# Routing: ScalarE scales x to unit length, and the normalised mu carries the router's scalar

## The chip, the cores and the metric

The kernel runs on one core of one Trainium2 chip. The metric is the device time of one execution in microseconds (us), the median over the runs. A core has five engines that work independently and wait for each other on semaphores: TensorE (PE in the profile, its weight loads PEld), VectorE (DVE), ScalarE (ACT), GpSimd (POOL) and SyncE (SP), which issues DMAs.

## The reference

Sixteen sequences of 256 tokens with 256 features pass through attention, a feed-forward block, a second attention, and a soft mixture of 16 experts with 16 slots each. Only the routing of the last block is touched by the change:

```python
xn = _layernorm(x, ln_gamma, ln_beta)
x_unit = _l2norm(xn, axis=-1)          # x / max(|x|, 1e-12)
mu_unit = _l2norm(mu, axis=0)
logits = jnp.einsum('bnd,des->bnes', x_unit * scale, mu_unit)
dispatch = jax.nn.softmax(logits, axis=1)
combine = jax.nn.softmax(logits.reshape(B, N, E * S), axis=-1).reshape(B, N, E, S)
slot_in = jnp.einsum('bnd,bnes->besd', xn, dispatch)
```

`scale` is one scalar. Here B = 16, N = 256, D = 256, E * S = 256.

## The kernel before, in words

The kernel is a row of stages: prologue, attention, feed-forward, attention, then `route`, `experts` and `combine`. All engines meet at a barrier between stages. `route` goes through the 16 sequences ("batches") one after another; the order of the work on each engine is written out by hand, and semaphores tie the engines together. A batch has its 256 tokens in two halves (q = 0, 1) of 128 partitions x 256 features.

For one batch the work goes through these tiles:

- VectorE: `ln.statistics` (route_stats, route_mean_var); GpSimd: `ln.inverse_deviation` (route_var_eps, route_rstd); VectorE: `ln.normalise` (route_xn, L351, two operations from SBUF to SBUF).
- GpSimd: `affine` (route_xg = xn * gamma, route_xa = xg + beta); ScalarE: `square` (route_sq with its sum); GpSimd: `lengths` (route_length, then route_length_min, L1744).
- VectorE: `unit`: route_inv_length, the reciprocal (L1641), then route_xu = xa * inv_length * scale (L1645, two operations from SBUF to SBUF).
- TensorE transposes xu (L1513). ScalarE rounds it to route_xT_hi (L1589), VectorE takes the rest, route_xT_lo (L1651). Every product on TensorE is made in three passes of such high and low parts.
- TensorE: `logits` for k = 0 (dispatch) and k = 1 (combine). VectorE: `maxima` (route_top, L1656); ScalarE: `exponentials` (route_ex, L1595); VectorE: `invert` (route_rinv) and `weigh` (route_weight, L1667).
- TensorE transposes the weights. ScalarE copies them: route_disp_hi (L1609) and moe_comb (L1614). VectorE: route_disp_lo (L1680). ScalarE and GpSimd split xa: `round_x` (route_xaS_hi) and `split_x` (route_xaS_lo, L1748). TensorE: `slot_inputs` (L1544). ScalarE: moe_slots (L1624).

The stages of this chain overlap over several batches. In one pass of a body, batch f is in front (logits and softmax), batch f - 1 at the back (dispatch and slots), batch f + 1 gets xu and xT, batch f + 2 gets xn, xa and its length, batch f + 3 its statistics. The bodies of f = 0 to 2 and of 13 to 16 stand outside the hardware loop, which runs two of them at a time for f = 3 to 12. The last bodies leave out the parts for batches that don't exist. Each engine's order in a body:

- VectorE: normalise (f + 2), maxima (f, 0), unit (f + 1), disp_lo (f - 1), statistics (f + 3), invert (f, 0), maxima (f, 1), xT_lo (f + 1), weigh (f, 0), invert (f, 1), weigh (f, 1).
- ScalarE: disp_hi (f - 1), exponentials (f, 0), comb (f - 1), xT_hi (f + 1), exponentials (f, 1), square (f + 2), slots (f - 1), round_x (f + 1).
- GpSimd: split_x (f), affine (f + 2), inverse_deviation (f + 3), lengths (f + 2).
- TensorE: logits (f, 0), transposed weights (f - 1), logits (f, 1), transposed x (f + 1), slot_inputs (f - 1).

Ahead of the bodies, mu is normalised once: VectorE builds the diagonal matrix route_mu_diag (L1707, two operations) from the identity and 1/|mu|, TensorE multiplies it with ones, so that every partition has the whole row of 1/|mu|, and VectorE multiplies mu with that row.

Of the kernel before, what the change touches and what calls it, by code (L numbers as in the profile page):

```python
# [49 lines left out]
def at_least(eng, sem, value):  # L50

    if not isinstance(value, int) or value > 0:
        eng.wait_ge(sem, value)
# [1386 lines left out]
def route(nc, d, st):  # L1440
# [7 lines left out]
    with ExitStack() as stack:  # L1448
# [126 lines left out]
        @block.scalar  # L1575
        def _(act):
            def square(f, i):

                act.wait_ge(xa_ready, f + 1)
                for q in range(NC):  # L1580
                    at_least(act, sumsq_ready, NC * f + q)
                    at_least(act, len_ready, f)
                    nc.scalar.activation(sq[:, :], xa[i][:, q, :], ACT.Square, accum_out=sumsq[:, q:q + 1]).then_inc(sumsq_ready, 1)

            def transposed_x(f, i):
                for c in range(DC):
                    act.wait_ge(xt_psum, DC * f + c + 1)
                    at_least(act, l_psum, 2 * (f - 1))
                    nc.scalar.copy(xT[i][0][:, c, :], x_bank[c][:, 0:N]).then_inc(xt_hi, 1)  # L1589

            def exponentials(f, k):
                act.wait_ge(top_ready, 2 * f + k + 1)
                at_least(act, weight_ready, 4 * (f - 1) + 2 * k + 2)
                for r in range(2):
                    nc.scalar.activation(ex[k][:, r, :], l_bank[k][:, r * ES:(r + 1) * ES], ACT.Exp,  # L1595
                                         bias=top[k][:, r:r + 1], accum_out=rsum[k][:, r:r + 1]).then_inc(ex_ready, 1)

            def round_x(f, i):

                at_least(act, i_psum, f - 1)  # L1600
                act.wait_ge(xa_ready, f + 1)
                nc.scalar.copy(xaS[i][0][:, :, :], xa[i][:, :, :]).then_inc(xas_hi, 1)

            def batch(f, i, front, back, following, later, latest):
                g = f - 1
                if back:
                    act.wait_ge(t_psum, 2 * g + 1)
                    at_least(act, i_psum, g)
                    nc.scalar.copy(disp[0][:, :, :], t_bank[0][:, :].rearrange("p (q n) -> p q n", q=NC)).then_inc(disp_hi, 1)  # L1609
                if front:  # L1610
                    exponentials(f, 0)
                if back:
                    act.wait_ge(t_psum, 2 * g + 2)
                    nc.scalar.copy(st.comb[:, :, bass.ds(g, 1), :].rearrange("p j b n -> p (j b) n"),  # L1614
                                   t_bank[1][:, :].rearrange("p (j n) -> p j n", j=EC)).then_inc(comb_stored, 1)
                if following:
                    transposed_x(f + 1, 1 - i)
                if front:
                    exponentials(f, 1)
                if later:  # L1620
                    square(f + 2, i)
                if back:
                    act.wait_ge(i_psum, g + 1)
                    nc.scalar.copy(st.slots[:, :, bass.ds(g, 1), :].rearrange("p c b n -> p (c b) n"),  # L1624
                                   i_bank[:, :].rearrange("p (c n) -> p c n", c=DC)).then_inc(slots_stored, 1)
                if following:
                    round_x(f + 1, 1 - i)

            square(0, 0)
            transposed_x(0, 0)  # L1630
            square(1, 1)
            round_x(0, 0)
            batch_pairs_ahead(act, batch)

        @block.vector
        def _(dve):
            def unit(f, i):

                dve.wait_ge(lmin_ready, f + 1)
                at_least(dve, xu_ready, NC * f)  # L1640
                nc.vector.reciprocal(inv_length[:, :], length_min[:, :]).then_inc(inv_ready, 1)  # L1641
                dve.wait_ge(inv_ready, f + 1)
                at_least(dve, xt_psum, DC * f)
                for q in range(NC):
                    nc.vector.tensor_scalar(xu[:, q, :], xa[i][:, q, :], inv_length[:, q:q + 1], scale[:, 0:1],  # L1645
                                            ALU.mult, ALU.mult).then_inc(xu_ready, 1)

            def transposed_x(f, i):
                for c in range(DC):
                    dve.wait_ge(xt_hi, DC * f + c + 1)  # L1650
                    nc.vector.tensor_tensor(xT[i][1][:, c, :], x_bank[c][:, 0:N], fp32_of(xT[i][0][:, c, :]),  # L1651
                                            ALU.subtract).then_inc(xt_lo, 1)

            def maxima(f, k):
                dve.wait_ge(l_psum, 2 * f + k + 1)
                nc.vector.tensor_reduce(top[k][:, :], l_bank[k][:, :].rearrange("p (r n) -> p r n", r=2), AX,  # L1656
                                        ALU.max, negate=True).then_inc(top_ready, 1)

            def invert(f, k):
                dve.wait_ge(ex_ready, 4 * f + 2 * k + 2)  # L1660
                nc.vector.reciprocal(rinv[k][:, :], rsum[k][:, :]).then_inc(rinv_ready, 1)

            def weigh(f, k):
                dve.wait_ge(rinv_ready, 2 * f + k + 1)
                at_least(dve, t_psum, 2 * (f - 1) + k + 1)
                for r in range(2):
                    nc.vector.tensor_scalar(weight[k][:, r, :], ex[k][:, r, :], rinv[k][:, r:r + 1], None,  # L1667
                                            ALU.mult).then_inc(weight_ready, 1)

            def batch(f, i, front, back, following, later, latest):  # L1670
                g = f - 1
                if later:
                    ln.normalise(dve, f + 2, xg_ready, 1)
                if front:
                    maxima(f, 0)
                if following:
                    unit(f + 1, 1 - i)
                if back:
                    dve.wait_ge(disp_hi, g + 1)
                    nc.vector.tensor_tensor(disp[1][:, :, :], t_bank[0][:, :].rearrange("p (q n) -> p q n", q=NC),  # L1680
                                            fp32_of(disp[0][:, :, :]), ALU.subtract).then_inc(disp_lo, 1)
                if latest:
                    ln.statistics(dve, f + 3)
                if front:
                    invert(f, 0)
                if front:
                    maxima(f, 1)
                if following:
                    transposed_x(f + 1, 1 - i)
                if front:  # L1690
                    weigh(f, 0)
                if front:
                    invert(f, 1)
                    weigh(f, 1)

            nc.vector.tensor_tensor(mu_sq[:, :, :], mu_raw[:, :, :], mu_raw[:, :, :], ALU.mult).then_inc(mu_step, 1)
            ln.statistics(dve, 0)
            dve.wait_ge(mu_psum, 1)
            nc.vector.tensor_copy(mu_sum[:, :], i_bank[:, 0:EC]).then_inc(mu_step, 1)
            ln.normalise(dve, 0, xg_ready, 1)  # L1700
            ln.statistics(dve, 1)

            dve.wait_ge(mu_pow, 2)
            nc.vector.reciprocal(mu_inv[:, :], mu_max[:, :]).then_inc(mu_step, 1)
            dve.wait_ge(mu_step, 3)
            for j in range(EC):
                last = nc.vector.tensor_scalar(mu_diag[:, j, :], st.ident[:, :], mu_inv[:, j:j + 1], None, ALU.mult)  # L1707
            last.then_inc(mu_step, 1)
            ln.normalise(dve, 1, xg_ready, 1)
            dve.wait_ge(mu_psum, 2)  # L1710
            nc.vector.tensor_tensor(mu_unit[:, :, :], mu_raw[:, :, :], l_bank[0][:, 0:ES].unsqueeze(1).to_broadcast([P, DC, ES]),
                                    ALU.mult).then_inc(mu_step, 1)
            dve.wait_ge(mu_step, 5)
            nc.vector.tensor_copy(mu[0][:, :, :], mu_unit[:, :, :]).then_inc(mu_step, 1)
            dve.wait_ge(mu_step, 6)
            nc.vector.tensor_tensor(mu[1][:, :, :], mu_unit[:, :, :], fp32_of(mu[0][:, :, :]), ALU.subtract).then_inc(mu_ready, 1)
            dve.wait_ge(in_, 48)
            ln.statistics(dve, 2)
            unit(0, 0)
            transposed_x(0, 0)  # L1720
            batch_pairs_ahead(dve, batch)

# [378 lines left out]
```

## Time and profile before

| | |
|---|---|
| median of 3 runs | 1213.59 us (1213.54, 1213.59, 1218.73) |
| profiled execution, its own time | 1216.6 us |
| its span | 1214.8 us |
| TensorE busy | 1047.5 us, 86% |
| VectorE busy | 894.0 us, 74% |
| ScalarE busy | 734.7 us, 60% |
| GpSimd busy | 439.4 us, 36% |
| granted TensorE clock, mean | 0.925 |
| routing stage | about 964 to 1119 us of the span |

The busy shares are means over all stages. A group of instructions is one line of the kernel with its output and inputs; its busy time is the sum of its instructions' durations. An instruction's duration contains the time for which it stands in the engine, whatever holds it there. Rows of one tile that follow each other directly are merged: "2.34 DVE ... x2" are two instructions that together take 2.34 us from the start of the first to the end of the second. In brackets stands how long the engine was idle before, and what released it.

### The profile page before, as it was taken

Reading aid. Unit: us, or ns where it says so; the run is one execution under the profiler, and the core shown is the slowest. Engines: PE = TensorE matmul, PEld = TensorE weight load, DVE = VectorE, ACT = ScalarE, POOL = GpSimd, SP = SyncE. Lnnn points to the kernel's source line nnn. Section 1 sums busy time; section 2 is a strip of 40 time slices with the busy share of each in tenths; the row PEclk is TensorE's granted clock in tenths of the full one; section 3 lists DMA queues with packets and bytes.
Section 4 is the critical chain, followed back from the end, with each engine's and each line's share of the span. In section 5 each row is a group of like instructions: output and inputs, shape, how many; then the busy total and the mean of one; then the engine's idle time right before and its main releaser. Section 6 shows DMA issues by size and latency. Waiting matters only on the chain. (4 is left out here: it accounts for less than half of the span.)

```text
span 1214.8 us, 28495 instructions
## 1 busy us (share of the span) xinstructions
PE 1047.5 (86%) x8053; PEld 998.5 (82%) x8053; DVE 894.0 (74%) x2324; ACT 734.7 (60%) x2481; POOL 439.4 (36%) x753
## 2 busy tenths in 40 slices
PE   6779999999999998799999917888888657777998
PEld 6679999999999998799999916888778646777777
DVE  3567667777767775677777647899998579996656
ACT  3466666676666665433333318899999346666754
POOL 0222323222232321121212126667776457663015
PEclk9889999999999999899999967899999769989559
DMA  7678970000000000000000045555664100000113
GB/s 223 144 134 227 130 117 0 0 0 0 0 0 0 0 1 1 31 1 0 0 0 0 0 108 150 150 159 161 175 172 128 19 1 1 0 0 2 42 35 121
DMA packets 71574, 73.90 MB, mean 61 GB/s; under 512 B 23024, under 2 KB 63828, under 8 KB 71380
## 3 DMA queue, kind: packets, MB, share of 16 engines
q1 hardware_dynamic: 70692, 72.47, 24.3%
q10 hardware_dynamic: 816, 0.66, 0.2%
q8 instruction: 28, 0.46, 0.2%
q14 instruction: 38, 0.31, 0.1%
HBM read 41.52 MB, written 31.54 MB: 60 GB/s over the span
## 5 line engine op out<-in xcount | busy, mean ns | idle before, releaser
L776 POOL TENSOR_TENSOR att_prob<-att_ex,att_rinv 128x308 f32<-128x308 f32 x128 | 90.0, 703 | 215.8 <-DVE att_rinv L679 202.5
L1056 ACT ACTIVATE att_ex<-att_s_bank,att_mx 128x77 f32<-128x77 f32 x512 | 144.3, 347 | 14.2 <-DVE att_mx L1122 12.7
L1338 ACT ACTIVATE ffn_hid<-ffn_h_bank,ffn_b 128x256 f32<-128x256 f32 x128 | 60.8, 476 | 125.5 <-DVE ffn_hT_lo L1369 64.8
L638 ACT ACTIVATE att_ex<-att_s_bank,att_mx 128x77 f32<-128x77 f32 x512 | 125.1, 333 | 11.5 <-DVE att_mx L669 11.4
L702 DVE TENSOR_TENSOR att_pT_lo<-att_t_bank,att_pT_hi 128x512 fp32r<-128x512 f32 x128 | 88.3, 690 | 33.2 <-ACT att_pT_hi L616 32.9
L646 ACT ACTIVATE att_qT<-att_q_bank 128x256 f32<-128x256 f32 x128 | 49.2, 385 | 100.3 <-PE att_q_bank L496 99.1
L1196 POOL TENSOR_TENSOR att_prob<-att_ex,att_rinv 128x256 f32<-128x256 f32 x128 | 80.3, 628 | 72.1 <-DVE att_rinv L1137 72.0
L516 PE MATMUL att_s_bank<-att_keys,att_qT 128*128 128x154 f32 x512 | 95.1, 309 | 0.0
L616 ACT CAST att_pT_hi<-att_t_bank 128x512 fp32r<-128x512 f32 x128 | 75.0, 587 | 24.6 <-PE att_t_bank L526 19.8
L540 PE MATMUL att_o_bank<-att_pT_hi,att_vals_hi 128*128 128x256 f32 x256 | 83.0, 324 | 3.0 <-DVE att_oT_lo L683 2.0
L1309 PE MATMUL ffn_o_bank<-ffn_w_hi,ffn_hT_hi 128*128 128x256 f32 x256 | 74.4, 291 | 7.6 <-DVE ffn_hT_lo L1369 7.6
L967 PE MATMUL att_s_bank<-att_ks,att_qs 100*128 100x154 f32 x256 | 52.6, 290 | 31.6 <-ACT att_ex L1056 20.9
L683 DVE TENSOR_TENSOR att_oT_lo<-att_o_bank,att_oT_hi 128x256 fp32r<-128x256 f32 x128 | 54.3, 424 | 33.3 <-ACT att_oT_hi L651 29.6
L496 PE MATMUL att_q_bank<-att_xT_hi,att_wq_hi 128*128 128x256 f32 x256 | 75.3, 294 | 2.9 <-DVE att_xT_lo L662 2.9
L526 PE MATMUL att_t_bank<-all_ident,att_prob 128*128 128x128 f32 x512 | 76.9, 273 | 0.0
L1296 PE MATMUL ffn_h_bank<-ffn_xT_hi,ffn_w_hi 128*128 128x256 f32 x256 | 72.8, 284 | 3.5 <-DVE ffn_xT_lo L1356 3.5
L1122 DVE TENSOR_REDUCE att_mx<-att_s_bank 128x4 f32<-128x308 f32 x128 | 59.7, 467 | 20.6 <-PE att_s_bank L967 20.2
L516 PEld LDWEIGHTS att_s_bank<-att_keys,att_qT 128*128 128x128 f32 x512 | 73.4, 193 | 1.1
L496 PE MATMUL att_q_bank<-att_xT_hi,att_wq_lo 128*128 128x256 f32 x256 | 73.1, 286 | 0.0
L496 PE MATMUL att_q_bank<-att_xT_lo,att_wq_hi 128*128 128x256 f32 x256 | 72.8, 284 | 0.0
L967 PEld LDWEIGHTS att_s_bank<-att_ks,att_qs 100*128 100x128 f32 x256 | 41.9, 204 | 37.4 <-DMA att_qs<-q_dram 29.1
L1296 PE MATMUL ffn_h_bank<-ffn_xT_lo,ffn_w_hi 128*128 128x256 f32 x256 | 72.5, 283 | 0.0
(275 smaller groups left out, 4162.6 us busy)
## 6 DMA issues: line engine op xcount, KB each, us to landing
att_qs<-q_dram SPq DMA_DIRECT2D x96, 128.0 KB, 2.8
ks_dram<-att_zeros SPq DMA_DIRECT2D x16, 462.0 KB, 5.7
att_ks<-ks_dram SPq DMA_DIRECT2D x16, 462.0 KB, 5.0
all_x<-in_x SPq DMA_DIRECT2D x4, 1024.0 KB, 7.1
att_vd<-vd_dram SPq DMA_DIRECT2D x16, 256.0 KB
q_dram<-att_qT_hi SPq DMA_DIRECT2D x16, 256.0 KB, 2.1
q_dram<-att_qT_lo SPq DMA_DIRECT2D x16, 256.0 KB, 2.1
out<-comb_y SPq DMA_DIRECT2D x16, 256.0 KB, 2.1
```

The lines of the kernel that those rows point to most:

```text
L496: last = nc.tensor.matmul(q_bank[c % 2][:, 0:N], wq[a][:, k, c * P:(c + 1) * P], xT[b][:, k, :], start=n == 0, stop=n == 5)
L516: last = nc.tensor.matmul(out, qT[c % 2][:, q * P:(q + 1) * P], keys[:, kc, h0:h0 + 2, :], start=first, stop=True)
L526: last = nc.tensor.transpose(t_bank[t % 2][:, h * N + q * P:h * N + (q + 1) * P], prob[:, q, (2 * t + h) * SK:(2 * t + h) * SK + P], st.id ...
L540: last = nc.tensor.matmul(o_bank[j % 2][:, 0:N], vals[a][:, v * P:(v + 1) * P], pT[t % 2][b][:, h * N:(h + 1) * N], start=t % PC == 0 and ...
L616: nc.scalar.copy(pT[t % 2][0][:, :], t_bank[t % 2][:, :]).then_inc(pt_hi, 1)
L638: last = nc.scalar.activation(ex[t % RING][:, r, :], s_bank[t % 2][:, r * SK:(r + 1) * SK], ACT.Exp, bias=mx[t % 2][:, r:r + 1])
L702: nc.vector.tensor_tensor(pT[t % 2][1][:, :], t_bank[t % 2][:, :], fp32_of(pT[t % 2][0][:, :]), ALU.subtract).then_inc(pt_lo, 1)
L776: nc.gpsimd.tensor_tensor(out, e, w, ALU.mult).then_inc(p_ready, 1)
L967: last = nc.tensor.matmul(s_bank[t % 2][:, q * PAIR:(q + 1) * PAIR], qs[i][0:ROWS, t, q * P:(q + 1) * P], ks[i][0:ROWS, t // 4, t % 4, :, ...
L1056: last = nc.scalar.activation(ex[t % RING][:, r, :], s_bank[t % 2][:, r * SK:(r + 1) * SK], ACT.Exp, bias=mx[t % 2][:, r:r + 1], **total)
L1196: nc.gpsimd.tensor_tensor(main, e[:, :, :, 0:MAIN], w.to_broadcast([P, NC, 2, MAIN]), ALU.mult).then_inc(p_ready, 1)
L1296: last = nc.tensor.matmul(h_bank[t % 4][:, 0:N], w1[a][:, k, t, :], xT[b][:, k, :], start=n == 0, stop=n == 5)
```

## The change

Three things change in `route`. The reciprocal stays on VectorE as `invert_length` and moves from behind the first maxima to the head of VectorE's body, ahead of normalise. The product with it goes to ScalarE as `unit`, two operations at the head of ScalarE's body, ahead of disp_hi. The router's scalar leaves this product: mu_diag is multiplied by it once, so VectorE waits for the small inputs' DMA ahead of mu_diag instead of ahead of the statistics of batch 2.

```diff
@@ ScalarE
+            def unit(f, i):
+                act.wait_ge(inv_ready, f + 1)
+                at_least(act, xt_psum, DC * f)
+                for q in range(NC):
+                    nc.scalar.mul(xu[:, q, :], xa[i][:, q, :], inv_length[:, q:q + 1]).then_inc(xu_ready, 1)
...
             def batch(f, i, front, back, following, later, latest):
                 g = f - 1
+                if following:
+                    unit(f + 1, 1 - i)
                 if back:
                     act.wait_ge(t_psum, 2 * g + 1)
...
             square(0, 0)
+            unit(0, 0)
             transposed_x(0, 0)
@@ VectorE
-            def unit(f, i):
+            def invert_length(f):
 
                 dve.wait_ge(lmin_ready, f + 1)
                 at_least(dve, xu_ready, NC * f)
                 nc.vector.reciprocal(inv_length[:, :], length_min[:, :]).then_inc(inv_ready, 1)
-                dve.wait_ge(inv_ready, f + 1)
-                at_least(dve, xt_psum, DC * f)
-                for q in range(NC):
-                    nc.vector.tensor_scalar(xu[:, q, :], xa[i][:, q, :], inv_length[:, q:q + 1], scale[:, 0:1],
-                                            ALU.mult, ALU.mult).then_inc(xu_ready, 1)
...
             def batch(f, i, front, back, following, later, latest):
                 g = f - 1
+                if following:
+                    invert_length(f + 1)
                 if later:
                     ln.normalise(dve, f + 2, xg_ready, 1)
                 if front:
                     maxima(f, 0)
-                if following:
-                    unit(f + 1, 1 - i)
...
             dve.wait_ge(mu_step, 3)
+            dve.wait_ge(in_, 48)
             for j in range(EC):
-                last = nc.vector.tensor_scalar(mu_diag[:, j, :], st.ident[:, :], mu_inv[:, j:j + 1], None, ALU.mult)
+                last = nc.vector.tensor_scalar(mu_diag[:, j, :], st.ident[:, :], mu_inv[:, j:j + 1], scale[:, 0:1],
+                                               ALU.mult, ALU.mult)
...
-            dve.wait_ge(in_, 48)
             ln.statistics(dve, 2)
-            unit(0, 0)
+            invert_length(0)
             transposed_x(0, 0)
```

## Rows read from the trace of the kernel before

**Rows 1.** Busy us by stretch: PE, PEld, DVE, ACT, POOL, granted clock, DMA share, GB/s

```profile
984.00:1110.00 126.00, 96.46 (x696) 89.44 (x696) 115.90 (x288) 79.74 (x262) 80.17 (x98) 0.92 0.00 1
```

**Rows 2.** Groups by form, 975 to 1120: busy us, mean ns, idle before

```profile
L1645 DVE TENSOR_SCALAR route_xu<-route_xa,route_inv_length,route_scale 128x256 f32<-128x256 f32 x32 | 35.7, 1154 | 0.6
...
L1583 ACT ACTIVATE route_sq<-route_xa 128x256 f32<-128x256 f32 x30 | 12.5, 416 | 0.5
...
L1589 ACT CAST route_xT_hi<-route_x_bank 128x256 fp32r<-128x256 f32 x32 | 10.6, 375 | 31.0 <-PE route_x_bank L1513 30.8
```

**Rows 3.** Waits from 984 to 1110: us in total, times, longest

```profile
DVE route_inv_length L1641 <- POOL route_length_min L1744: 2.4, 7, 0.5
```

**Rows 4.** Timeline of VectorE, 1034 to 1062: start, duration in us

```profile
1036.90 0.17 DVE L1641 RECIPROCAL route_inv_length<-route_length_min 128x2 f32<-128x2 f32 x1 [0.36 <-POOL route_length_min L1744]
1037.10 2.34 DVE L1645 TENSOR_SCALAR route_xu<-route_xa,route_inv_length,route_scale 128x256 f32<-128x256 f32 x2
1039.36 0.68 DVE L1680 TENSOR_TENSOR route_disp_lo<-route_t_bank,route_disp_hi 128x512 fp32r<-128x512 f32 x1
...
1041.64 0.74 DVE L1651 TENSOR_TENSOR route_xT_lo<-route_x_bank,route_xT_hi 128x256 fp32r<-128x256 f32 x2
...
1045.62 2.68 DVE L1645 TENSOR_SCALAR route_xu<-route_xa,route_inv_length,route_scale 128x256 f32<-128x256 f32 x2
1048.22 0.68 DVE L1680 TENSOR_TENSOR route_disp_lo<-route_t_bank,route_disp_hi 128x512 fp32r<-128x512 f32 x1
```

**Rows 5.** Timeline of GpSimd, batches 0 and 1, and three in the loop

```profile
984.41 1.28 POOL L1748 TENSOR_TENSOR route_xaS_lo<-route_xa,route_xaS_hi 128x512 fp32r<-128x512 f32 x1
...
993.39 0.22 POOL L1744 TENSOR_SCALAR route_length_min<-route_length 128x2 f32<-128x2 f32 x1
...
1036.56 0.22 POOL L1744 TENSOR_SCALAR route_length_min<-route_length 128x2 f32<-128x2 f32 x1 [0.29 <-ACT route_xaS_hi L1602]
1036.73 1.29 POOL L1748 TENSOR_TENSOR route_xaS_lo<-route_xa,route_xaS_hi 128x512 fp32r<-128x512 f32 x1
1037.98 1.31 POOL L1729 TENSOR_TENSOR route_xg<-route_xn,route_gamma 128x512 f32<-128x512 f32 x1
...
1045.06 0.22 POOL L1744 TENSOR_SCALAR route_length_min<-route_length 128x2 f32<-128x2 f32 x1 [0.29 <-POOL route_length L1741]
1045.60 1.28 POOL L1748 TENSOR_TENSOR route_xaS_lo<-route_xa,route_xaS_hi 128x512 fp32r<-128x512 f32 x1 [0.32 <-issue]
...
1053.95 0.22 POOL L1744 TENSOR_SCALAR route_length_min<-route_length 128x2 f32<-128x2 f32 x1 [0.29 <-ACT route_xaS_hi L1602]
```

**Rows 6.** Timeline of ScalarE: second exponentials of a batch, and disp_hi

```profile
1041.84 0.47 ACT L1595 ACTIVATE route_ex<-route_l_bank,route_top 128x256 f32<-128x256 f32 x1 [1.15 <-DVE route_top L1656]
...
1044.69 0.59 ACT L1609 CAST route_disp_hi<-route_t_bank 128x512 fp32r<-128x512 f32 x1
```

**Rows 7.** Timeline of VectorE, start of the stage and batches 0 and 1

```profile
969.25 0.48 DVE L1707 TENSOR_SCALAR route_mu_diag<-all_ident,route_mu_inv 128x128 f32<-128x128 f32 x2
973.79 0.73 DVE L351 TENSOR_SCALAR route_xn<-all_x,route_mean_var,route_rstd 128x256 f32<-128x256 f32 x2 [4.06 <-POOL route_rstd L343]
...
984.48 1.68 DVE L351 TENSOR_SCALAR route_xn<-all_x,route_mean_var,route_rstd 128x256 f32<-128x256 f32 x2 [2.71 <-POOL route_rstd L343]
986.09 0.68 DVE L1656 TENSOR_REDUCE route_top<-route_l_bank 128x2 f32<-128x512 f32 x1
...
986.87 2.13 DVE L1645 TENSOR_SCALAR route_xu<-route_xa,route_inv_length,route_scale 128x256 f32<-128x256 f32 x2
...
989.84 0.67 DVE L1656 TENSOR_REDUCE route_top<-route_l_bank 128x2 f32<-128x512 f32 x1
...
994.20 0.69 DVE L1656 TENSOR_REDUCE route_top<-route_l_bank 128x2 f32<-128x512 f32 x1 [1.13 <-PE route_l_bank L1523]
...
997.50 0.68 DVE L1680 TENSOR_TENSOR route_disp_lo<-route_t_bank,route_disp_hi 128x512 fp32r<-128x512 f32 x1
```

**Rows 8.** Timeline of VectorE, body 14, near the stage's end

```profile
1105.62 0.69 DVE L1656 TENSOR_REDUCE route_top<-route_l_bank 128x2 f32<-128x512 f32 x1 [2.16 <-PE route_l_bank L1523]
```

## The prediction

> **What bounds the kernel now.** I read the page first, then the busy time by stretch, then the groups and waits of the routing stage, and last its timeline engine by engine. The page's busy shares are a mean over stages with different limits, and its chain that ended last lies wholly in the combine stage at the end, so neither says anything about routing. The stretch from 984 to 1110 us does: VectorE is busy 115.9 of 126 us, TensorE 96.5, GpSimd 80.2, ScalarE 79.7 [rows 1]. VectorE is the full engine there, and its largest group in the stage is the very product that is to leave it: 32 operations, 35.7 us, 1154 ns each in the mean [rows 2]. A ScalarE operation on a tile of the same 128x256 takes 375 to 416 ns [rows 2].
>
> Why 1154 ns? The timeline tells. At 1037.10 two such products start; they end at 1039.44, 2.34 us for the pair [rows 4], while GpSimd runs route_xaS_lo from 1036.73 to 1038.02 and then route_xg to 1039.29 [rows 5]. The pair ends 0.15 us after GpSimd's second operation. The next batch repeats it: start 1045.62 against GpSimd's 1045.60, 2.68 us [rows 4, 5]. The pair at 986.87, with less cover from GpSimd, takes 2.13 us [rows 7]. So the product stands behind GpSimd: each of its two operations lasts until one of GpSimd's 1.3 us operations is over. The same befalls route_xn, another VectorE product from SBUF to SBUF: beside the route_xaS_lo of 984.41 to 985.69 its pair takes 1.68 us and ends 0.47 us after it [rows 7].
>
> The Trainium skill ("SBUF — State Buffer", Who interferes with whom) says that VectorE's two-port operations and GpSimd's take one shared pair of ports as an exclusive lock, and that issue order decides who blocks. The overlaps just read agree with it.
>
> **The loop that repeats.** route_disp_lo starts at 1039.36; the second maximum and xT_lo follow; ScalarE's second exponentials start at 1041.84 [rows 4, 6]; then ScalarE's squares, GpSimd's length, and its minimum route_length_min at 1045.06, route_xaS_lo at 1045.60, and the next disp_lo at 1048.22 [rows 4, 5]. Minimum to minimum is 8.50 us, then 8.89 [rows 5], 8.70 in the mean. disp_lo starts 1.34 us after route_xaS_lo ends in both (1038.02 to 1039.36, 1046.88 to 1048.22), because the product's pair ends 0.15 us after route_xg. The reciprocal route_inv_length already waits for that minimum in 7 batches, though two other VectorE operations, xn and the first maximum, stand ahead of it [rows 3].
>
> **Part 1, the product leaves VectorE.** Two operations a batch, 35.7 us in all. What that is worth is not 35.7 us but what the loop gives back, below.
>
> **Part 2, the reciprocal goes to the head of VectorE's batch.** Behind it wait xn, the first maximum, disp_lo and statistics, and everything after them. The minimum comes when it came before, since ScalarE's squares and GpSimd's order ahead of it are untouched. In the loop the reciprocal starts 0.34 us after the minimum's start (1036.56 to 1036.90) [rows 4, 5], so xn starts at about +0.5 (all such times count from the start of route_length_min), and GpSimd's route_xaS_lo starts at +0.17 (1036.73) or +0.54 (1045.60) [rows 5]. xn now lies where the product lay, and is held by the same operation. It is held once only: route_xg reads xn and can't start before it. From the row at 984.48, the pair ends 0.47 us after route_xaS_lo; the maximum starts 0.07 before that end (986.09), lasts 0.68, and the operation behind it can start 0.08 before it ends [rows 7]. disp_lo therefore starts 0.47 - 0.07 + 0.68 - 0.08 = 1.00 us after route_xaS_lo instead of 1.34: **0.34 us a batch**. VectorE will stand idle for some 1.6 us at the head of each batch: the 0.3 us by which it waits now [rows 3], and the 1.3 us that xn and the maximum, about 0.65 each to the next operation, now fill.
>
> **Part 3, ScalarE gets the product.** The trace has no ScalarE product with a scale per partition from SBUF. Bounds: route_xT_hi at 375 ns below, route_ex, which has a bias per partition, at 470 above [rows 2, 6]; I take 0.45, 0.9 us for the pair (the value between them that is nearer to the one with an operand per partition). It starts when the reciprocal is over, at +0.6, so ends at +1.5. disp_hi, now behind it, takes 0.59 [rows 6], to +2.1. disp_lo needs it at +0.17 + 1.29 + 1.00 = +2.46: hidden, with 0.35 us to spare. The exponentials then wait for the first maximum, which ends at +2.5. They (0.95), the copy of the combine weights (0.6) and the first half of xT_hi (0.35) end at about +4.4; xT_lo wants that half at 2.46 + 2.28 = +4.74 [rows 4], and the second exponentials want ScalarE at 2.46 + 2.48 = +4.94 [rows 4, 6]: hidden, 0.3 us to spare. TensorE's transposes get xu two us earlier, which gains nothing, as the slot products behind them wait for disp_lo. If the cover were gone the pair would cost its 0.9 us a batch.
>
> The Trainium skill ("ScalarE: Activation LUTs", What ACT_TABLE_LOAD costs) gives an operation with one pointer operand about 280 ns + 0.833 ns an element. An estimate from it is 0.49 us, 0.08 more for the pair than by the rows, and still covered.
>
> **Part 4, the scalar on mu.** Two operations on route_mu_diag get a second scalar; 0.48 us for both as now. They start at 969.25 and also wait for a DMA that is now waited for later. VectorE's next operation waits for GpSimd 4.06 us until 973.79 [rows 7]; so even if the DMA lands 4 us later than the two operations now start, that wait covers it. I take 0.
>
> **Start and end of the stage.** Batch 0: the product (986.87, 2.13 us) falls away between the maximum (ends 986.77) and the statistics; the second maximum, at 989.84, then has only to wait for the first exponentials, which follow the first maximum at 986.8 and take 0.95. It starts at about 987.95: 1.9 us [rows 7]. Batch 1: the minimum of 993.39 [rows 5], 1.9 us earlier, is at about 991.5, its route_xaS_lo ends 0.17 + 1.28 later at 992.95, disp_lo can start at 993.95 instead of 997.50 [rows 7]. TensorE's first logits, for which the maximum of 994.20 waited [rows 7], are done 1.9 us earlier too, by 992.3, and don't hold it. That is 3.5 us in all after batch 1, and that wait of 1.13 us is the larger part of the second step. Batches 2 to 13: 12 x 0.34 = 4.1. In batches 14 to 16 there is no xn and TensorE is the bound: the maximum at 1105.62 waited 2.16 us for it [rows 8], so nothing more comes.
>
> **Sum.** 3.5 + 4.1 = 7.6 us. The profiled execution took 1216.6 (span 1214.8, 1.8 around it) and would take 1209.0; it lies 3.0 over the median of the runs, 1213.59, from which I get **1206.0**. It is -0.63%; a measurement of this kernel can tell about 0.5% (6.1 us) from no change.
>
> **Rivals.** *A, 0.60: the forecast above*, with its own range of 1203 to 1209 (0.2 to 0.45 a batch, 2.5 to 4.5 at the start).
> *B, 0.17: the gain of the steady batches is eaten* and only the start remains, 1210, no change. ScalarE's chain through the first exponentials to xT_hi has 0.3 us of slack in my sum. If ScalarE or TensorE (whose transposes feed xT_hi, and which has spells at the low clock) is later by 0.3 + 0.34 us than I count, xT_lo moves past where it is now and the 12 x 0.34 are gone. For it: in the stage TensorE is granted 0.92 of its clock, not all of it [rows 1]. Against it: ScalarE's operations follow each other without gaps when their inputs are there.
> *C, 0.15: more gain, 1201.5.* In every second batch xn (+0.5) and route_xaS_lo (+0.54) are a tie [rows 5]; in it the product at 1045.62 lost. If xn starts first and is then not held, its pair takes some 0.74 us, disp_lo waits only for disp_hi at +2.1 instead of +2.82, and 6 batches gain 0.7 more: 4.3 us. Against it: in the tie at 1045.60 GpSimd's operation kept its 1.28 us and VectorE's waited, and route_xaS_lo can still slip in between the two operations of xn and hold the second one. (The Trainium skill, the same section as above: whoever issues first holds the pair for its whole instruction.)
> *D, 0.08: slower, 1223.* ScalarE's product is itself held by GpSimd as VectorE's was. With the 2.68 us of the longest pair [rows 4] xu ends at 0.6 + 2.68 = +3.3 and disp_hi at +3.9, so disp_lo starts at +3.9 where it now starts at +2.80; 12 batches lose 1.1 us each, the start gives 3.5, 1213.6 + 13.2 - 3.5 = 1223. It decides where the pair takes 2.4 us, 1.2 an operation: disp_lo at +3.6, 9.6 - 3.5 = 6.1 us lost. Against it: ScalarE's square of the same tile has a mean of 416 ns over 30 [rows 2].
>
> Faster by over 0.5%: four fifths of A and all of C, 0.62. Within: the rest of A, B, 0.30. Slower: 0.08. The range 1200 to 1212 takes in A, B and most of C, and leaves out D.
>
> **What would show it.** xu on ScalarE at 0.40 to 0.50 us, gapless pair. On VectorE: the reciprocal waits for the minimum in nearly every batch, about 1.5 us; xn's pair takes 1.5 to 1.7 us wherever it overlaps route_xaS_lo, and disp_lo starts 1.0 us after that ends. Minimum to minimum 8.35 us in the mean. The second maximum of batch 0 at 988. The prediction is wrong if xn isn't held (C), if xT_lo waits for xT_hi (B), or if the product on ScalarE lasts over 1 us (D).

## The result, and the profile after

The changed kernel is faster by 0.6%: ratio to before 0.9939, 95% interval 0.9925 to 0.9953, with medians of 1210.27 us against 1217.36 us over 20 runs each. (Two of the three runs of before that the prediction had, and so their median, lay at the lower end of those 20.) The forecast was 0.63% and 1206.0 us. On a second chip the ratio was 0.9912 (0.9894 to 0.9931); the two intervals just overlap.

The profiled execution has a span of 1206.2 us (before 1214.8) and took 1208.0. To see what the routing stage itself does, I take its length as the time from GpSimd's first operation in it (route_ones) to TensorE's first in the experts' stage (exp_b_bank): 1111.48 - 964.01 = 147.5 us after, 1120.15 - 964.60 = 155.6 us before. The stage is 8.1 us shorter and accounts for all of the gain but 0.6 us, which lies ahead of it. This length is a finer measure than the whole time. In the 13 profiles of this study the stage begins anywhere from 958.8 to 967.4 us, although nothing ahead of it was changed.

Busy time in the stretch that answers to [rows 1] (PE, PEld, DVE, ACT, POOL, granted clock, DMA share, GB/s):

```profile
984.00:1102.00 118.00, 90.84 (x699) 82.61 (x699) 92.46 (x258) 91.64 (x291) 79.49 (x97) 0.99 0.00 1
```

No engine is full any more. VectorE fell from 92% to 78%, ScalarE rose from 63% to 78%. The granted clock of TensorE rose too, from 0.92 to 0.99, and could be thought to be what gains. It doesn't set the loop: in the kernel before, two batches take 17.42 us at a granted clock of 1.00 (the minima of 1019.14 and 1036.56) and 17.40 at 0.90 (1045.06 and 1062.46). It does touch the last bodies: in that profile the granted clock is 0.50 from 1102 to 1104 us, the lower of its two levels, after TensorE had been busy for only 0.5 of the 2 us from 1098, and VectorE then waits 2.16 us for TensorE's logits [rows 8]. Experiment 1 has the same loop, a granted clock of 1.00 there and a wait of 0.52 us, and from the last minimum to the stage's end it takes 14.7 us in place of 15.7. About 1 us of the 8.1 may thus be that spell and not the change. The groups of the stage (busy us, mean ns of one, idle before), first xn's of the kernel before, then three of after:

```profile
L351 DVE TENSOR_SCALAR route_xn<-all_x,route_mean_var,route_rstd 128x256 f32 x20 | 7.3, 409 | 0.3
...
L351 DVE TENSOR_SCALAR route_xn<-all_x,route_mean_var,route_rstd 128x256 f32 x20 | 15.0, 790 | 0.8
L1589 ACT ACTIVATE route_xu<-route_xa,route_inv_length 128x256 f32<-128x256 f32 x32 | 14.6, 502 | 16.4 <-DVE route_inv_length L1650 16.4
...
L1650 DVE RECIPROCAL route_inv_length<-route_length_min 128x2 f32<-128x2 f32 x16 | 2.6, 164 | 22.9 <-POOL route_length_min L1749 22.9
```

The product that lasted 1154 ns on VectorE [rows 2] lasts 502 on ScalarE. But xn, which in the loop lasted 409 ns, now lasts 790, and VectorE stands idle for 22.9 us ahead of the reciprocal, where it waited 2.4 us before [rows 3]. VectorE's timeline shows where both come from:

```profile
1031.21 0.17 DVE L1650 RECIPROCAL route_inv_length<-route_length_min 128x2 f32<-128x2 f32 x1 [1.60 <-POOL route_length_min L1749]
1031.40 1.41 DVE L351 TENSOR_SCALAR route_xn<-all_x,route_mean_var,route_rstd 128x256 f32 x2
1032.73 0.68 DVE L1660 TENSOR_REDUCE route_top<-route_l_bank 128x2 f32<-128x512 f32 x1
1033.33 0.68 DVE L1684 TENSOR_TENSOR route_disp_lo<-route_t_bank,route_disp_hi 128x512 fp32r<-128x512 f32 x1
...
1039.38 0.17 DVE L1650 RECIPROCAL route_inv_length<-route_length_min 128x2 f32<-128x2 f32 x1 [1.70 <-POOL route_length_min L1749]
1039.67 1.63 DVE L351 TENSOR_SCALAR route_xn<-all_x,route_mean_var,route_rstd 128x256 f32 x2
1041.23 0.68 DVE L1660 TENSOR_REDUCE route_top<-route_l_bank 128x2 f32<-128x512 f32 x1
1041.83 0.67 DVE L1684 TENSOR_TENSOR route_disp_lo<-route_t_bank,route_disp_hi 128x512 fp32r<-128x512 f32 x1
```

And GpSimd's, with which it is to be read:

```profile
1030.87 0.22 POOL L1749 TENSOR_SCALAR route_length_min<-route_length 128x2 f32<-128x2 f32 x1 [0.29 <-ACT route_xaS_hi L1608]
1031.05 1.28 POOL L1753 TENSOR_TENSOR route_xaS_lo<-route_xa,route_xaS_hi 128x512 fp32r<-128x512 f32 x1
1033.08 1.27 POOL L1734 TENSOR_TENSOR route_xg<-route_xn,route_gamma 128x512 f32<-128x512 f32 x1 [0.75 <-DVE route_xn L351]
...
1039.03 0.22 POOL L1749 TENSOR_SCALAR route_length_min<-route_length 128x2 f32<-128x2 f32 x1 [0.29 <-POOL route_length L1746]
1039.56 1.28 POOL L1753 TENSOR_TENSOR route_xaS_lo<-route_xa,route_xaS_hi 128x512 fp32r<-128x512 f32 x1 [0.31 <-issue]
1041.58 1.26 POOL L1734 TENSOR_TENSOR route_xg<-route_xn,route_gamma 128x512 f32<-128x512 f32 x1 [0.75 <-DVE route_xn L351]
...
1047.57 0.22 POOL L1749 TENSOR_SCALAR route_length_min<-route_length 128x2 f32<-128x2 f32 x1 [0.29 <-ACT route_xaS_hi L1608]
```

route_xaS_lo ends at 1032.33 and at 1040.84. xn's pair ends 0.48 and 0.46 us later, disp_lo starts 1.00 and 0.99 us later, in place of 1.34 before [rows 4, 5]. From minimum to minimum it is 8.16 and 8.54 us, 8.35 in the mean, in place of 8.70.

### The profile page after: what moved, and what is told of

Its sections match the earlier page's. It is cut to its first block and busy times, and to the rows that moved or that the text cites. A ratio compares the mean times of both kernels' runs of the same rounds, so it can differ in the third digit from the quotient of the medians.

```text
span 1206.2 us, 28505 instructions
## 1 busy us (share of the span) xinstructions
PE 1040.5 (86%) x8053; PEld 988.6 (82%) x8053; DVE 874.2 (72%) x2292; ACT 748.9 (62%) x2513; POOL 437.8 (36%) x753
```

## The experiments

The theory under test, below the **loop theory**: a batch lasts as long as the loop that runs from route_length_min over whatever VectorE has beside GpSimd's 1.3 us operations, then disp_lo, the second maxima, ScalarE's exponentials and squares, back to the next minimum; a tensor_scalar of VectorE from SBUF to SBUF (the products, xn, the weights) that meets one of them is held until that is over. The rivals are that the time follows the engines' load (work taken off the full engine is what gains, wherever it stands), that ScalarE is the new bound, and that the early reciprocal is what gains. The kernels of a group shared a chip and its runs of before: changed again, 1, 2 and 3; then 4 to 7; then 9, 7 again and 8. "Stage" is the length defined above, "two batches" the time between every second route_length_min in the loop (before 17.39 us); for 8, 9 and the second run of 7 it is taken from one route_length to the second after it, which has the same period.

| kernel | ratio to before, 95% | stage us | two batches us |
|---|---|---|---|
| before | 1 | 155.6 | 17.39 |
| changed, again | 0.9912 (0.9894 to 0.9931) | 147.5 | 16.70 |
| 1 only the scalar moves | 0.9988 (0.9969 to 1.0007) | 154.0 | 17.39 |
| 2 reciprocal back behind the maxima | 0.9880 (0.9862 to 0.9899) | 140.1 | 15.45 |
| 3 route_xaS_lo behind route_xg | 0.9878 (0.9858 to 0.9898) | 143.2 | 16.13 |
| 4 ScalarE's product behind the exponentials | 1.0046 (1.0027 to 1.0065) | 161.9 | 18.40 |
| 5 ScalarE's product made twice | 0.9952 (0.9934 to 0.9970) | 150.7 | 17.06 |
| 6 as 2, product behind the exponentials | 0.9814 (0.9793 to 0.9836) | 134.2 | 14.24 |
| 7 as 2, product behind disp_hi | 0.9818 (0.9794 to 0.9841) | 131.7 | 14.24 |
| 7 again | 0.9806 (0.9781 to 0.9831) | 132.5 | 14.23 |
| 8 as 7, minimum on VectorE | 0.9821 (0.9802 to 0.9839) | 135.7 | 14.28 |
| 9 before, both at the head of VectorE | 1.0011 (0.9993 to 1.0029) | 156.8 | 17.98 |

### The changed kernel again

> The changed kernel itself, to have it on the same chip as the next three. 0.61% faster than before, about 7.5 us, under every theory; it is the mark for the others.

The stage is 147.5 us long, as in the first profile; the ratio is 0.3% lower than there. So 8 of the about 10.7 us (0.9912 of 1215.5) are the stage's; the other 2.7 lie in stages that both kernels have alike, and I don't claim them for the change.

### Experiment 1: the scalar alone

```diff
-nc.vector.tensor_scalar(xu[:, q, :], xa[i][:, q, :], inv_length[:, q:q + 1], scale[:, 0:1],
-                        ALU.mult, ALU.mult).then_inc(xu_ready, 1)
+nc.vector.tensor_scalar(xu[:, q, :], xa[i][:, q, :], inv_length[:, q:q + 1], None,
+                        ALU.mult).then_inc(xu_ready, 1)
```

(and the changed kernel's lines for mu_diag)

> Kernel before, in which only the scalar has moved into mu_diag; VectorE keeps the product, with one scalar operand instead of two. Loop theory (a batch lasts from one route_length_min over route_xaS_lo, the held product, disp_lo and the second maxima to the next): no change, within 0.2% of before, since the product's pair ends with GpSimd's route_xg and not by its own work; the pair stays at 2.1 to 2.7 us in the loop. Rival, that the second scalar operand makes the product slow: the pair falls towards 0.74 us and the kernel gains as much as the whole change or more.

No change: 0.9988, the interval holds 1. Two batches take 17.39 us as before; the stage is 1.6 us shorter, 1.0 of it behind the last minimum, where the kernel before had its spell at the low clock, and 0.3 ahead of the first. The product with one scalar lasts as long as with two:

```profile
L1645 DVE TENSOR_SCALAR route_xu<-route_xa,route_inv_length 128x256 f32<-128x256 f32 x32 | 36.5, 1181 | 0.6
```

The second operand is not what makes it slow, and this part of the change gives nothing in the loop and nothing that the whole time can show.

### Experiment 9: the place alone

```diff
 def batch(f, i, front, back, following, later, latest):      # VectorE, before
     g = f - 1
+    if following:
+        unit(f + 1, 1 - i)
     if later:
         ln.normalise(dve, f + 2, xg_ready, 1)
     if front:
         maxima(f, 0)
-    if following:
-        unit(f + 1, 1 - i)
```

> Kernel before, in which only the place has changed: reciprocal and product, both still on VectorE, stand at the head of its body, ahead of xn and the first maximum. Loop theory: the product's first operation is held by route_xaS_lo, its second is free, because route_xg now waits for the xn behind it; the pair falls to about 1.6 us, ends 0.47 us after route_xaS_lo, then xn (0.65) and the maximum (0.60) come into the loop: disp_lo starts 1.7 us after route_xaS_lo ends instead of 1.34. 0.3 us a batch lost, 12 batches 4 us, less what the start gives or takes: 0.1 to 0.5% slower than before. So the early place alone costs, and the gain of the change is that of ScalarE's taking the product. Rival, that starting the reciprocal early is what gains: 0.3 to 0.6% faster than before.

The ratio, 1.0011, can't be told from 1; the loop can. Two batches take 17.98 us (from 1040.93 to 1058.91; before 17.39), so 0.3 us a batch are lost, as expected. The product's pair is here beside route_xaS_lo alone and is held once; xn behind it has no GpSimd operation beside it and takes its own 0.72 us:

```profile
1041.28 0.17 DVE L1641 RECIPROCAL route_inv_length<-route_length_min 128x2 f32<-128x2 f32 x1 [1.70 <-POOL route_length_min L1744]
1041.48 1.72 DVE L1645 TENSOR_SCALAR route_xu<-route_xa,route_inv_length,route_scale 128x256 f32<-128x256 f32 x2
1043.13 0.72 DVE L351 TENSOR_SCALAR route_xn<-all_x,route_mean_var,route_rstd 128x256 f32 x2
```

route_xaS_lo ran from 1041.46 to 1042.73 there, the pair ended 0.47 us later; its mean over the stage is 755 ns in place of 1154. 0.3 us a batch, lost twelve times, is 3.6 us; the stage is only 1.2 us longer, as the start gains 2.9 (in the bodies of f = 0 and 1 the minima come 8.4 and 8.1 us apart in place of 10.3 and 9.2). The early reciprocal by itself doesn't gain in the loop: that rival is out.

### Experiment 2: the reciprocal back behind the maxima

```diff
 def batch(f, i, front, back, following, later, latest):      # VectorE, changed
     g = f - 1
-    if following:
-        invert_length(f + 1)
     if later:
         ln.normalise(dve, f + 2, xg_ready, 1)
     if front:
         maxima(f, 0)
+    if following:
+        invert_length(f + 1)
```

> Changed kernel, with the reciprocal put back behind the first maxima (the product stays on ScalarE). Loop theory: xn and the first maximum again fill the wait for route_length_min and no longer overlap route_xaS_lo, so xn's pair falls to 0.74 us; disp_lo then waits only for disp_hi, at +2.1 after the minimum's start instead of +2.46 and +2.80. 0.5 us a batch, 6 us, so 1.1% faster than before and minimum to minimum about 7.85 us. Rival, that the whole gain is the work taken off VectorE wherever the reciprocal stands, or that ScalarE is what bounds the changed kernel: the same time as the changed kernel, 0.6% faster than before.

1.2% faster than before, 0.3% more than the changed kernel on the same chip, and the stage 7.4 us shorter than the changed kernel's; two batches take 15.45 us, 7.73 for one where 7.85 were expected. VectorE's timeline of one batch:

```profile
1050.97 0.73 DVE L351 TENSOR_SCALAR route_xn<-all_x,route_mean_var,route_rstd 128x256 f32 x2
1051.62 0.68 DVE L1660 TENSOR_REDUCE route_top<-route_l_bank 128x2 f32<-128x512 f32 x1
1052.59 0.17 DVE L1650 RECIPROCAL route_inv_length<-route_length_min 128x2 f32<-128x2 f32 x1 [0.29 <-POOL route_length_min L1749]
1054.29 0.69 DVE L1684 TENSOR_TENSOR route_disp_lo<-route_t_bank,route_disp_hi 128x512 fp32r<-128x512 f32 x1 [1.53 <-ACT route_disp_hi L1617]
```

ScalarE's timeline of the same batch:

```profile
1052.88 0.91 ACT L1589 ACTIVATE route_xu<-route_xa,route_inv_length 128x256 f32<-128x256 f32 x2 [0.90 <-DVE route_inv_length L1650]
1053.69 0.56 ACT L1617 CAST route_disp_hi<-route_t_bank 128x512 fp32r<-128x512 f32 x1
```

xn and the maximum are done before the minimum, xn at its own 0.73 us. Now disp_lo waits 1.53 us for disp_hi, which stands behind ScalarE's product: the next wait in the row, at +2.05 after the minimum of 1052.24. The instructions of every engine are those of the changed kernel, so the theory that load alone counts is out.

### Experiment 3: route_xaS_lo behind route_xg

```diff
 def batch(f, i, front, back, following, later, latest):      # GpSimd, changed; affine in two
+    if later:
+        scaled(f + 2)        # route_xg
     if front:
         split_x(f, i)        # route_xaS_lo
     if later:
-        affine(f + 2, i)
+        shifted(f + 2, i)    # route_xa
```

> Changed kernel, with GpSimd's route_xaS_lo moved from ahead of route_xg to between route_xg and route_xa. route_xg needs xn, so GpSimd runs nothing large beside xn. If xn is held by GpSimd's operation, its pair falls from 1.4 to 1.7 us to 0.74 us, and disp_lo waits only for disp_hi at +2.1: 0.3 to 0.5 us a batch, 4 to 6 us, 0.9 to 1.1% faster than before; part may be lost again as route_xa ends later, which ScalarE's squares read. If xn is slow for itself (two scalar operands, its place), the pair stays at 1.4 us or more and the time at that of the changed kernel or slower.

1.2% faster than before, the stage 4.3 us shorter than the changed kernel's. The loop gains 0.28 us a batch on the changed kernel's, a little less than the 0.3 to 0.5 expected; the ratio is over the expected one because the changed kernel's is on this chip as well. VectorE's order is untouched, and xn's pair is free at once; the weights are held in its place:

```profile
1048.17 1.03 DVE L1671 TENSOR_SCALAR route_weight<-route_ex,route_rinv 128x256 f32<-128x256 f32 x2
...
1051.62 0.17 DVE L1650 RECIPROCAL route_inv_length<-route_length_min 128x2 f32<-128x2 f32 x1 [1.69 <-POOL route_length_min L1755]
1051.92 0.74 DVE L351 TENSOR_SCALAR route_xn<-all_x,route_mean_var,route_rstd 128x256 f32 x2
```

This is the cleanest test of the hold: the same instruction in the same place of VectorE's row, 0.74 us without GpSimd beside it and 1.41 to 1.63 with. The weights' pair went from 0.61 to 1.03 us, since GpSimd's route_xa (1047.52 to 1048.79) now ran beside it. The Trainium skill ("SBUF — State Buffer", Who interferes with whom) names tensor_scalar among the VectorE operations whose two-port modes can take the pair of ports shared with GpSimd. This trace agrees for the two tensor_scalars here, xn and the weights.

### Experiment 4: ScalarE's product behind the exponentials

```diff
 def batch(f, i, front, back, following, later, latest):      # ScalarE, changed
-    if following:
-        unit(f + 1, 1 - i)
...
     if front:
         exponentials(f, 0)
+    if following:
+        unit(f + 1, 1 - i)
```

> Changed kernel, with ScalarE's product moved from the head of its body to behind the first exponentials; the reciprocal stays at VectorE's head. Loop theory: the exponentials still wait for the held xn and the maximum (until +2.5), xu ends at +4.3, TensorE's transposes at +5.0, xT_hi's first half at +5.4 where xT_lo wants it at +4.74; a batch lasts 0.6 to 0.8 us longer, 8 to 10 us, so the gain is gone: between 0.2% slower and 0.1% faster than before. Rival, that only the load of the engines counts: the same time as the changed kernel.

Slower than before, 1.0046 (1.0027 to 1.0065): more than expected. Two batches take 18.40 us in the mean, 0.85 us a batch over the changed kernel where 0.6 to 0.8 were forecast. The place of the wait is the expected one:

```profile
1055.57 0.85 DVE L1655 TENSOR_TENSOR route_xT_lo<-route_x_bank,route_xT_hi 128x256 fp32r<-128x256 f32 x2 [0.90 <-ACT route_xT_hi L1595]
```

So ScalarE's product is hidden in the changed kernel by its place, not by ScalarE's having room.

### Experiment 5: ScalarE's product made twice

```diff
     for q in range(NC):
         nc.scalar.mul(xu[:, q, :], xa[i][:, q, :], inv_length[:, q:q + 1]).then_inc(xu_ready, 1)
+    for q in range(NC):
+        nc.scalar.mul(spare[:, q, :], xa[i][:, q, :], inv_length[:, q:q + 1])
```

> Changed kernel, with ScalarE's two products made once more into a spare tile, right behind the first two and ahead of disp_hi (nobody reads them). It measures the cover over ScalarE's product. Loop theory: 0.85 us more ahead of disp_hi, which ends at +2.9 instead of +2.05, so disp_lo at +2.95 instead of +2.46 and +2.80: 0.15 to 0.5 us a batch, 4 us, 0.3% slower than the changed kernel; half of the added work is covered. If ScalarE is the bound: all 16 x 0.85 = 13 us come on top, 0.5% slower than before. If ScalarE has room: no change against the changed kernel.

The stage is 3.2 us longer than the changed kernel's, two batches 17.06 in place of 16.70 us, 0.18 a batch. (The changed kernel wasn't run on this chip, so the stages are compared and not the ratios.) 16 x 0.8 = 13 us were added to ScalarE, and three quarters of it cost nothing. ScalarE doesn't bound the changed kernel, but the cover over disp_hi is thin: in the changed kernel disp_hi ends at 1032.80 and disp_lo starts at 1033.33, 0.5 us to spare where 0.35 were summed. With 0.8 us more, disp_lo waits for disp_hi in one of two batches:

```profile
1048.87 0.69 DVE L1687 TENSOR_TENSOR route_disp_lo<-route_t_bank,route_disp_hi 128x512 fp32r<-128x512 f32 x1 [0.21 <-ACT route_disp_hi L1620]
```

The minimum there is at 1046.11, so disp_lo starts at +2.76 in place of +2.46; in the other batch it is +2.85 in place of +2.80.

### Experiments 6 and 7: both moves together

Experiment 2's VectorE, with ScalarE's product behind the first exponentials (6) or right behind disp_hi (7).

```diff
 def batch(f, i, front, back, following, later, latest):      # ScalarE, experiment 7
-    if following:
-        unit(f + 1, 1 - i)
...
+    if following:
+        unit(f + 1, 1 - i)
     if front:
         exponentials(f, 0)
```

> The last two together: reciprocal behind the first maxima, ScalarE's product behind the first exponentials. Loop theory: the first maximum is done before the minimum, disp_hi at -0.3, disp_lo at +0.55 instead of +2.46 and +2.80, exponentials +0.2 to +1.15, xu to +2.0, xT_hi to +3.5, second exponentials at +3.5 instead of about +5.1. The chain alone gives 6.7 us from minimum to minimum; GpSimd's own row of work with its gaps gives about 7.0 to 7.1 and becomes the bound. 1.25 us a batch over the changed kernel, 15 us: 1.7 to 2.0% faster than before. Rival, that ScalarE bounds the changed kernel already: no more than 0.6 to 0.8% faster than before.

> As the run before, but with the product between disp_hi and the first exponentials. disp_lo at +0.55 as there, but the first exponentials at +1.5 to +2.45, so the second maximum stands behind a reciprocal that waits until +2.5 and ends at +3.3; second exponentials at +3.7. Chain 6.9 us, GpSimd 7.0 to 7.1: 1.6 to 1.9% faster than before, equal to the run before or 0.1% behind it.

> Reciprocal behind the first maxima and ScalarE's product between disp_hi and the exponentials once more, as the mark for the run after it on the same chip: 1.8% faster than before.

1.9%, 1.8% and again 1.9% faster than before, on two chips; by the ratio 6 and 7 can't be told apart. Their loops are equally long, and the stage of 7 is 1.8 to 2.5 us shorter by its start. Minimum to minimum is 7.12 us, as GpSimd's row of work gave. Its timeline in the second run of 7:

```profile
1035.43 0.22 POOL L1749 TENSOR_SCALAR route_length_min<-route_length 128x2 f32<-128x2 f32 x1 [0.29 <-POOL route_length L1746]
1035.96 1.28 POOL L1753 TENSOR_TENSOR route_xaS_lo<-route_xa,route_xaS_hi 128x512 fp32r<-128x512 f32 x1 [0.32 <-issue]
1037.20 1.29 POOL L1734 TENSOR_TENSOR route_xg<-route_xn,route_gamma 128x512 f32<-128x512 f32 x1
1038.93 1.27 POOL L1740 TENSOR_TENSOR route_xa<-route_xg,route_beta 128x512 f32<-128x512 f32 x1 [0.43 <-POOL route_xg L1734]
1040.29 0.37 POOL L340 TENSOR_SCALAR route_var_eps<-route_mean_var 128x2 f32<-128x2 f32 x1
1040.84 0.71 POOL L343 TENSOR_TENSOR route_rstd<-route_var_eps,all_minus_half 128x2 f32<-128x2 f32 x1 [0.18 <-POOL route_var_eps L340]
1041.70 0.85 POOL L1746 TENSOR_TENSOR route_length<-route_sumsq,route_half 128x2 f32<-128x2 f32 x1
1042.84 0.22 POOL L1749 TENSOR_SCALAR route_length_min<-route_length 128x2 f32<-128x2 f32 x1 [0.29 <-POOL route_length L1746]
```

No other engine ends any gap in this row: they are GpSimd's own waits for its last result, and starts. Both versions beat the kernel before and the changed one clearly, with the changed kernel's instructions in another order.

### Experiment 8: the minimum on VectorE

```diff
-    nc.gpsimd.tensor_scalar(length_min[:, :], length[:, :], NORM_EPS, None, ALU.max).then_inc(lmin_ready, 1)
...
 def invert_length(f):                                         # VectorE
+    dve.wait_ge(len_ready, f + 1)
+    nc.vector.tensor_scalar(length_min[:, :], length[:, :], NORM_EPS, None, ALU.max).then_inc(lmin_ready, 1)
     dve.wait_ge(lmin_ready, f + 1)
```

> As the run before, and in addition the 128x2 operation route_length_min moves from GpSimd to VectorE, right ahead of the reciprocal. If GpSimd's row of work bounds that kernel (7.1 us from minimum to minimum, as seen), it loses 0.22 us of work and the 0.3 us gap ahead of it: 6.6 to 6.9 us, 2 to 6 us in all, 1.95 to 2.3% faster than before. If the chain through VectorE and ScalarE or TensorE bounds it instead, VectorE gets 0.2 us more: no change or 0.1% slower than the run before.

Missed: no gain, which the expectation had named as the sign that GpSimd's row is not the bound. The ratio is 0.9821 beside 0.9806, the loop is as long as without it (14.28 us for two batches against 14.23), the stage 3 us longer. The operation that was to be small isn't, in one batch of two:

```profile
1037.34 1.02 DVE L1649 TENSOR_SCALAR route_length_min<-route_length 128x2 f32<-128x2 f32 x1
...
1044.65 0.16 DVE L1649 TENSOR_SCALAR route_length_min<-route_length 128x2 f32<-128x2 f32 x1
```

At 1037.34 it meets route_xaS_lo (1037.05 to 1038.34) and is held for it, with the reciprocal, xu and disp_lo behind it; in the other batch GpSimd now waits 1.33 us for ScalarE's squares. GpSimd lost 0.5 us of work and the loop found another way round of the same length. The hold confounds the test, so it doesn't decide. That GpSimd's row bounds experiment 7 is read from a row in which no other engine's work is waited for, but not shown by taking work away. What the loop's limit is with the minimum on VectorE and no hold on it wasn't tried.

## Why the prediction was right

**VectorE was the full engine, through the held product.** Right: the product with one scalar is as slow (experiment 1), and next to nothing but route_xaS_lo it falls from 1154 to 755 ns (experiment 9). That a full engine is not by itself what the time follows was right too: of some 2.5 us a batch taken off VectorE the loop gave back 0.35.

**Part 2, xn takes the product's place in the hold: 0.34 us a batch.** Right in mechanism and size: disp_lo starts 1.00 and 0.99 us after route_xaS_lo where 1.00 was summed, minimum to minimum fell from 8.70 to 8.35 us, and VectorE stands idle 1.6 to 1.7 us at the head where 1.6 was summed. Experiment 3 took the hold away and got xn's 0.74 us back; experiment 2 took xn out of the loop. Of the three parts of the change the early place is the one that speaks against it: alone it costs 0.3 us a batch (experiment 9), and undone it gives 7.4 us of stage (experiment 2). The other part, the product on ScalarE, gives 15.4 us of stage without it (experiment 2); the change as made keeps 8.1.

**Part 3, ScalarE's product under cover.** Right, closely: 0.91 us for the pair where 0.9 was summed, and ScalarE idle for 0.23 to 0.28 us ahead of the second exponentials, where 0.3 us to spare were summed. One operation lasts 502 ns against the 0.45 that I took from the rows, and the second starts before the first has ended, so the pair takes 0.91. The estimate of 0.49 us from the Trainium skill ("ScalarE: Activation LUTs", What ACT_TABLE_LOAD costs) is closer for one operation: the trace has 502 ns. xu reaches TensorE 1.4 to 1.7 us earlier than before, counted from the minimum, not two. Experiment 5 shows the cover's depth and experiment 4 what it costs without: 0.85 us a batch, about the pair's 0.9.

**Part 4, the scalar on mu.** The sum's 0 holds, the working doesn't. The two operations on mu_diag did not last 0.48 us as before but 2.65: the wait for the DMA moved them beside GpSimd's route_xg and route_xa, and they were held.

```profile
969.20 1.26 POOL L1734 TENSOR_TENSOR route_xg<-route_xn,route_gamma 128x512 f32<-128x512 f32 x1 [1.36 <-DMA route_scale<-in_L_ffn_scale]
969.23 2.65 DVE L1712 TENSOR_SCALAR route_mu_diag<-all_ident,route_mu_inv,route_scale 128x128 f32<-128x128 f32 x2 [0.69 <-DMA route_scale<-in_L_ffn_scale]
```

The 4.06 us of idle time that was to cover a late DMA [rows 7] covered this too: 1.05 us of it were left.

**Start and end.** Counted from the start of the stage, the second maximum of batch 0 starts 2.0 us earlier (987.24), where 1.9 were summed, and disp_lo of batch 1 3.7 us earlier (993.22), where 3.5 were. The minimum of the fourth batch comes 24.5 us after the first where it was 27.9 before: 3.4 us for a forecast 3.5. From there to the fifteenth the loop gives 94.84 - 90.83 = 4.0 us, for a forecast 4.1. What lies ahead of the first minimum gives 0.3 us, which nothing in the sum had; experiment 1 has it too, so it comes with the scalar's move or by chance. What follows the fifteenth minimum gives 0.35, and that is rather the clock's than the change's: against experiment 1, where the wait of 2.16 us at the end [rows 8] is only 0.52, the same piece of the changed kernel is 0.7 us longer. So the sum's nothing for the last bodies rests on a wait that was long in a profile with a spell at the low clock. Together 8.1 us, forecast 7.6.

**The rivals.** B (ScalarE's chain eats the gain) didn't come, but experiment 4 shows how near it lies. C (xn wins the tie against route_xaS_lo) didn't come either: in the batches of the tie xn started at 1039.67, 0.11 us after route_xaS_lo, not 0.04 ahead of it. D (GpSimd holds ScalarE as well) is out: 502 ns in the mean of 32 and 514 at most, with route_xaS_lo beside nearly all of them.

**The time.** 1210.3 us lies in the range of 1200 to 1212 but 4 us over the forecast, because the three runs of before on which it was built were low by 3.8 against the 20; the ratio, 0.9939 for a forecast 0.9937, is what hits. That it hits so closely is in part luck: about 1 us of the stage's 8.1 may be the clock's, and on the second chip the ratio is 0.9912.

**Small slips that change nothing.** The 0.08 us by which the operation behind the maximum can start before its end isn't in the rows cited for it: 986.77 to 986.87 is a gap, with the reciprocal at 986.69 between, which does start 0.08 us early. By the chances given, faster by over 0.5% sums to 0.63 and within to 0.29, not 0.62 and 0.30, and C's own gain gives 1201.7 us.

## What to carry to other kernels

Where a VectorE tensor_scalar from SBUF to SBUF lasts a multiple of its twins, look for a GpSimd operation beside it and see whether the two end together; what pays then is to take it out of GpSimd's way, and one of its kind that moves into its place is held in turn, as xn and the weights were. Work taken from a full engine is worth what the repeating loop gives back, here 0.35 of 2.5 us a batch; to find it, follow the loop from one late result to the next and ask what VectorE does while it waits. An early wait at the head of an in-order row costs all that stands behind it: with the same instructions, waits placed behind ready work gave three times the gain in the stage (experiment 7, 23 to 24 us against 8.1).

## What the runs showed of the hardware that was not expected

A VectorE tensor_scalar on 128x2 elements is held like a large one: 1.02 us beside GpSimd's route_xaS_lo, 0.16 without (experiment 8). Two of 128x128 that take 0.48 us alone took 2.65 beside two of GpSimd's in a row. But not every VectorE operation from SBUF to SBUF is held: in the changed kernel the reciprocal of the same 128x2 ran at 1031.21 beside route_xaS_lo and took 0.17 us, and none of the 16 took more; the statistics' pair at 1033.93 started beside route_xg and took 0.74 us, and its operations lie between 400 and 415 ns in all 28. ScalarE's products showed nothing of it. And the stages ahead of the changed one, alike in all kernels, ended anywhere in 8.6 us from profile to profile, more than the whole effect; the length of the stage itself repeated to 0.1 us (147.5 and 147.5) and 0.8 us (131.7 and 132.5), but a spell at the low clock can add 1 us to it, as in the profile of before.
